# Sampling stage in loops, causal filter merged with the step sizes, a scan product on VectorE

## The chip, the cores and the metric

The kernel runs on one core of a Trainium2 chip. The metric is the device time of one execution in microseconds. TensorE (PE) multiplies, VectorE (DVE), ScalarE (ACT) and GpSimd (POOL) do the element work, and SyncE (SP) issues most transfers.

## The reference

Two layers work on an image x of shape (2, 128, 64, 64).

Layer 0 normalises over the channels and runs four deformable convolutions with kernels 1, 1, 3 and 7 wide, together 60 taps. Every tap samples the image at a learned place:

```python
offset = conv2d(x, off_w, off_b, pad)
mask = 2.0 * jax.nn.sigmoid(conv2d(x, mod_w, mod_b, pad))
py = base_y + off[:, :, 0]
px = base_x + off[:, :, 1]
sampled = bilinear_sample(x, py, px) * mask[:, None]
return jnp.einsum('bckhw,ock->bohw', sampled, reg_w.reshape(O, C, k * k))
```

The offsets and masks come from ordinary convolutions. The four results and a pooled branch are normalised and fused, and a mixture of 8 experts follows.

Layer 1 normalises, projects to 512 channels, filters them with a 5x5 depthwise kernel, and applies channel and spatial attention. Half of the channels (256) go through a causal filter of four taps along the 4096 positions, SiLU, and a selective scan with 16 states: delta = softplus(projection), state = exp(delta * A) * state + delta * u * B, y = sum over states of C * state. The result is gated and projected, and a layer of 64 specialists closes.

## The kernel before

**Sampling.** `deformable` takes the 8192 positions in 16 groups of 512 (four tiles of 128). For each of the 60 taps of a group, GpSimd issues four indirect gathers (L641) of table rows into one of four corner slots. VectorE and ScalarE weigh the four corners and add them up (L671 to L687 on VectorE, L953 on ScalarE), TensorE transposes the result (`turn`, L868), ScalarE copies that to SBUF (L961, `operands`), and TensorE multiplies it with the tap's weights (`multiply`, L879), which SyncE loads tap by tap (L580). Multiplication runs two taps behind (LAG). VectorE lists the row numbers of a later tap (L695, `list_rows`), on which GpSimd's next gathers wait.

In between, the positions of later groups are made: ScalarE stages seven shifted patches of a strip (`stage`), TensorE filters them with the 49 taps of the offset and mask convolution (`convolve`, L856), ScalarE sorts the sums (`sort`), and VectorE computes positions, indices, factors and weights at fixed taps. The order on every engine is written out by hand: constants such as SORT_AT, STAGE_AT and CONV_AT say behind which tap each step stands. `group_loop` unrolls the 16 groups; within one, two short loops (LOOPS) cover taps 2 to 25 and 26 to 45. TensorE's program is unrolled over all groups and taps:

```python
for half, c in ((0, g + 2), (1, g + 1), (1, g + 2)):
    begin, end = CONV_AT[half]
    ...
    if c < GROUPS and begin <= at < end:
        convolve(c, half, at - begin, end - begin)
```

Group 15 leaves out what would prepare a next group, and group 14 half of it.

**Layer 1.** For each of the two batches, `causal` loads all of u (two halves of 2 MB), filters it on VectorE (L2149 the first tap, L2152 the others) and applies SiLU on ScalarE (L2164). Its block ends, and `step_sizes` starts: in eight chunks of 512 positions TensorE projects, ScalarE makes exp and log (softplus), VectorE replaces the log by a polynomial where the argument is small (L2324 to L2336), forms delta (L2339) and delta * u (L2345), and TensorE and ScalarE turn the product into `dut`. Then `scan` goes over 4 chunks of 1024 positions times 16 states, 64 steps: ScalarE scales eight tiles of `dut` by B (L2422) and makes two decays (L2427), TensorE turns the products into the drive (L2506), VectorE scans both halves (L2477) and keeps the carries (L2462), GpSimd multiplies with C (L2444), and TensorE adds up (L2520). VectorE keeps the chunk's sum with L2467.

## Time and profile before

| | us |
|---|---|
| median of 3 runs (lowest, highest) | 9125.77 (9112.52, 9134.54) |
| the profiled execution | 9135.6 |
| its span | 9133.6 |
| mean granted TensorE clock | 0.812 |
| sampling stage (207 to 6600) | 6393 |
| causal filter and step sizes, batch 0 (7710 to 7860) | 150 |
| scan, batch 0 (7860 to 8209) | 349 |

The time is that of the whole execution, the span that from the first to the last instruction. A busy share tells how long an engine worked; idle time of an engine means something only where others wait for it.

### The profile page before, as it was taken

The numbers are of one execution on the slowest core, as the hardware profiler recorded it, in microseconds if no ns is written. First come the engines' busy times: TensorE is split into PE (matmuls) and PEld (weight loads), VectorE is DVE, ScalarE is ACT, GpSimd is POOL, SyncE is SP. The second block draws the span as 40 slices with busy tenths as digits, with TensorE's granted clock in tenths as the row PEclk, the third lists the DMA queues.
The fourth block names the chain that finished last, engine by engine and source line by source line (L and its number), as shares of the span: only waits on it lengthen the run. The fifth ranks groups of instructions, "written<-read, shape, count | busy, mean of one in ns | idle before, by whom it ended". The sixth has DMA issues, their size and how long they took to land. (4 is left out here: it accounts for less than half of the span.)

```text
span 9133.6 us, 99111 instructions
## 1 busy us (share of the span) xinstructions
PE 5511.6 (60%) x22734; PEld 3442.0 (38%) x22734; DVE 5304.2 (58%) x10463; ACT 4537.0 (50%) x11966; POOL 4809.8 (53%) x4571
## 2 busy tenths in 40 slices
PE   4665555555555555555556565554478985665757
PEld 4433333333333333333333333322235432462644
DVE  3454554555555555545555555555527886887962
ACT  1444444544444454444445444444452664895940
POOL 1555555655556565555556565555500884481830
PEclk9877777878788788777777787777799997896977
DMA  6565666666666666655566666666640001131234
GB/s 167 168 194 169 180 181 180 189 179 191 180 190 186 182 194 189 182 172 177 169 182 192 181 198 182 183 185 196 180 157 27 28 28 38 57 107 68 99 134 149
DMA packets 587069, 1413.87 MB, mean 155 GB/s; under 512 B 93923, under 2 KB 258032, under 8 KB 581616
## 3 DMA queue, kind: packets, MB, share of 16 engines
q0 software_dynamic: 308224, 1006.95, 37.7%
q1 hardware_dynamic: 276210, 398.68, 13.7%
q10 hardware_dynamic: 2304, 4.20, 0.1%
q8 instruction: 164, 2.69, 0.1%
q14 instruction: 167, 1.37, 0.1%
HBM read 1323.03 MB, written 85.86 MB: 154 GB/s over the span
## 5 line engine op out<-in xcount | busy, mean ns | idle before, releaser
L641 POOL DMA_INDIRECT st_corners<-corner_table,df_rows x3840 | 3648.5, 950 | 2809.2 <-DVE df_rows L695 1562.2
L868 PE MATMUL df_turn_ps<-main_ident,df_sampled 128*128 128x128 f32 x3840 | 729.2, 322 | 2667.4 <-ACT df_turned L961 1353.0
L879 PE MATMUL df_acc_ps<-df_turned,df_tapw 128*128 128x512 f32 x3840 | 2100.3, 675 | 90.0 <-issue 43.3
L682 DVE TENSOR_TENSOR st_corners<-st_corners,df_part_ps 128x512 f32<-128x512 f32 x960 | 660.6, 688 | 2550.4 <-ACT df_part_ps L953 1969.4
L961 ACT ACTIVATE df_turned<-df_turn_ps 128x512 f32<-128x512 f32 x962 | 562.8, 585 | 2512.6 <-remote 2049.8
L868 PEld LDWEIGHTS df_turn_ps<-main_ident,df_sampled 128*128 128x128 f32 x3840 | 515.3, 164 | 3412.8 <-issue 1857.5
L953 ACT ACTIVATE df_part_ps<-st_corners,df_share 128x128 f32<-128x128 f32 x3840 | 1191.2, 356 | 401.6 <-DVE df_sampled L687 236.7
L953 ACT ACTIVATE st_corners<-st_corners,df_share 128x128 f32<-128x128 f32 x3840 | 1218.9, 391 | 43.1 <-DMA st_corners<-corner_table,df_rows 24.7
L856 PE MATMUL df_conv_ps<-st_ow,df_patch 128*128 128x147 f32 (+1 forms) x6272 | 1150.8, 338 | 26.9 <-issue 26.9
L856 PEld LDWEIGHTS df_conv_ps<-st_ow,df_patch 128*128 128x128 f32 x6272 | 1048.7, 230 | 35.0 <-issue 34.2
L879 PEld LDWEIGHTS df_acc_ps<-df_turned,df_tapw 128*128 128x128 f32 x3840 | 783.8, 223 | 707.7 <-issue 634.5
L2444 POOL TENSOR_TENSOR sc_read<-sc_state,sc_c_row 128x1024 f32<-128x1024 f32 x256 | 601.3, 2372 | 476.3 <-DVE sc_state L2477 409.3
L687 DVE TENSOR_TENSOR df_sampled<-st_corners,df_part_ps 128x512 f32<-128x512 f32 x960 | 660.3, 688 | 287.8 <-remote 182.3
L677 DVE TENSOR_TENSOR df_part_ps<-st_corners,df_weight_ps 128x512 f32<-128x512 f32 x960 | 683.2, 712 | 39.1 <-issue 39.1
L671 DVE TENSOR_TENSOR st_corners<-st_corners,df_weight_ps 128x512 f32<-128x512 f32 x960 | 653.8, 681 | 26.7 <-issue 12.0
L683 DVE TENSOR_TENSOR df_part_ps<-st_corners,df_part_ps 128x512 f32<-128x512 f32 x960 | 661.6, 689 | 0.0
L2477 DVE TENSOR_TENSOR_SCAN sc_state<-sc_decay,sc_carry,sc_drive_ps 128x1024 f32<-128x1024 f32 x256 | 594.1, 2341 | 68.9 <-PE sc_drive_ps L2506 44.4
L1843 PE MATMUL dw_conv_ps<-dw_padded,dw_diag 128*128 128x512 f32 x1024 | 471.3, 613 | 12.1 <-DVE dw_u L1968 12.1
L1953 DVE SCALAR_TENSOR_TENSOR dw_conv_ps<-dw_padded,dw_dw_w,dw_conv_ps 128x512 f32<-128x512 f32 x576 | 383.4, 749 | 104.4 <-PE dw_conv_ps L1843 104.4
L1821 POOL TENSOR_TENSOR dw_aside<-dw_aside,dw_scaled 128x512 f32<-128x512 f32 x320 | 407.3, 1273 | 47.6 <-POOL dw_aside L1821 1.3
L2422 ACT ACTIVATE sc_product<-l1i_dut,l1s_bt 128x256 f32<-128x256 f32 x1024 | 421.0, 494 | 0.5 <-DVE sc_a L2456 0.5
L2506 PE MATMUL sc_drive_ps<-main_ident,sc_product 128*128 128x128 f32 x2048 | 278.0, 280 | 207.6 <-ACT sc_product L2422 195.5
(319 smaller groups left out, 5537.7 us busy)
## 6 DMA issues: line engine op xcount, KB each, us to landing
df_tapw<-in_tap_w_dram SPq DMA_DIRECT2D x962, 128.0 KB
sc_c_row<-c SPq DMA_DIRECT2D x128, 512.0 KB, 3.7
st_corners<-corner_table,df_rows POOLq DMA_INDIRECT x3840
y_b<-df_y SPq DMA_DIRECT2D x128, 256.0 KB, 2.7
f_y_in<-y_b SPq DMA_DIRECT2D x128, 256.0 KB, 4.1
l1f_w<-in_w_dram SPq DMA_DIRECT2D x32, 1024.0 KB, 6.9
corner_table<-st_corners SPq DMA_DIRECT2D x16, 1024.0 KB
u<-dw_u SPq DMA_DIRECT2D x64, 256.0 KB, 2.1
```

The costliest lines, as they stand in the source:

```text
L641: nc.gpsimd.indirect_dma_start(corners[slot][:, j].rearrange("p v c -> p (v c)"), None, table, bass.IndirectOffsetOnAxis(ap=rows[slot][:, ...
L671: nc.vector.tensor_tensor(near, near, w[:, :, 0:2, :], ALU.mult).then_inc(weighed_v, 1)
L677: nc.vector.tensor_tensor(part_ps[:, 0:VT], corners[slot][:, 0:VT, 2:4, :], w[:, :, 2:4, :], ALU.mult).then_inc(weighed_v, 1)
L682: nc.vector.tensor_tensor(left, left, part_ps[:, :, 0, :], ALU.add).then_inc(paired, 1)
L683: nc.vector.tensor_tensor(part_ps[:, :, 1, :], corners[slot][:, :, 1, :], part_ps[:, :, 1, :], ALU.add).then_inc(paired, 1)
L687: nc.vector.tensor_tensor(sampled[pair][:], left, part_ps[:, :, 1, :], ALU.add).then_inc(summed, 1)
L856: m = nc.tensor.matmul(conv_ps[:, second, 0:n], patch[:, kx, row * W:(row + 2) * W], ow_sb[:, ky, kx, 0:n], start=False, stop=closes, skip ...
L868: t = nc.tensor.transpose(turn_ps[pair][:, j * TILE:(j + 1) * TILE], sampled[pair][:, j, :], ident[:])
L879: m = nc.tensor.matmul(acc_ps[:, h, :], tapw[pair][:, h * P:(h + 1) * P], turned_sb[pair][:], start=first, stop=last, skip_group_check=not ...
L953: nc.scalar.activation(dst, src, ACT.Copy, scale=share[slot][:, j - VT, v:v + 1]).then_inc(weighed_a, 1)
L2444: nc.gpsimd.tensor_tensor(read[2 * s + h][:], state[2 * s + h][:], c_row[s][:], ALU.mult).then_inc(read_done, 1)
L2477: v.tensor_tensor_scan(out=state[2 * s + h][:], data0=decay[2 * s + h][:], data1=drive_ps[h][:], initial=carry[:, bass.ds(n, 1), h], op0=A ...
```

## The change

The sampling stage's groups become loops on every engine, eight pairs of groups, with the taps' loops inside. TensorE gets a loop over 16 groups with three taps, a loop of two halves of 22 taps, and 11 taps. It filters for the next group, one half of the strip in each half of the stretch, in 18 taps each, one output row at a time, and waits once for all seven patches. The multiplications of the last two taps come at the end of their own group, before the next group's first turn. Sorting, staging and counting stand at other taps, the strip is loaded later in the group, and the last groups are no longer exempt. `causal` and `step_sizes` become one block, `filter_and_steps`: u comes in quarters, SiLU of the first quarter is followed by the first two chunks' projections, the polynomial lies in PSUM, and GpSimd forms delta * u. In the scan VectorE scales the eighth tile of each state, two states ahead.

```diff
-    SORT_AT = (53, 6 * SLOTS + 1)
-    STAGE_AT = (6 * SLOTS + 1, 54)
+    SORT_AT = (6 * SLOTS + 1, 11 * SLOTS + 1)
+    STAGE_AT = {1: 6 * SLOTS + 1, 0: 52}
-    CONV_AT = {0: (27, 53), 1: (-5, 25)}
-    POSITION_AT, INDEX_AT, FACTOR_AT, COUNT_AT, WEIGHT_AT = 47, 49, 51, 53, 56
+    STRETCH, HEAD, SHARES = 22, 3, 9
+    POSITION_AT, INDEX_AT, COUNT_AT, FACTOR_AT, WEIGHT_AT = 47, 49, 51, 53, 56
...
-            for g in range(GROUPS):
-                ring = g % 2
-                tap = 0
+            with eng.Fori(0, GROUPS // 2) as q:
+                with eng.Fori(0, 2) as ring:
+                    g = 2 * q + ring
+                    tap = 0
...
             def serve(b, gl, nb, ngl):
 
                 g = b * GPB + gl
-                if nb < B:
-                    sp.wait_ge(strip_free, g + 2)
-                    load_strip(nb, ngl)
                 tap = LAG
...
                     tap += rounds * SLOTS
+                sp.wait_ge(strip_free, g + 2)
+                load_strip(nb, ngl)
                 for tap in range(tap, TAPS):
...
-                if g + 1 == GROUPS:
-                    return
...
-            def convolve(c, half, part, parts):
+            def convolve(c, half, second, part, parts):
+
+                share = -(-len(conv_taps) // parts)
+                if part == 0:
+                    if not second:
+                        pe.wait_ge(patched, KMAX * (2 * c + half + 1))
...
+                for ky, kx in conv_taps[part * share:(part + 1) * share]:
...
+            with pe.Fori(0, GROUPS) as g:
+                for tap in range(HEAD):
                     turn(g, tap, tap % 2)
...
                     if tap >= LAG:
                         known(g, tap - LAG)
...
+                with pe.Fori(0, 2) as half:
+                    for u in range(STRETCH):
+                        pair = (HEAD + u) % 2
+                        tap = half * STRETCH + (HEAD + u)
+                        turn(g, tap, pair)
+                        if 2 <= u < 2 + 2 * SHARES:
+                            convolve(g + 1, half, (u - 2) // SHARES, (u - 2) % SHARES, SHARES)
+                        multiply(g, tap - LAG, pair, g * (TAPS // 2) + half * (STRETCH // 2) + (HEAD + u - LAG) // 2)
+                for tap in range(HEAD + 2 * STRETCH, TAPS):
+                    turn(g, tap, tap % 2)
+                    known(g, tap - LAG)
+                for tap in range(TAPS - LAG, TAPS):
+                    known(g, tap)
...
-def causal(nc, tag, d, b, u_dram, conv1_sb, xs_sb):
...
-def step_sizes(nc, tag, d, b, ident, xs_sb, delta_sb, dut_sb, bt_sb, c_dram):
+def filter_and_steps(nc, tag, d, b, ident, u_dram, conv1_sb, xs_sb, delta_sb, dut_sb, bt_sb, c_dram):
...
-        poly = [sb(f"poly{h}", [P, SPAN]) for h in range(HALVES)]
+        poly = [pb(f"poly{h}", [P, SPAN]) for h in range(HALVES)]
...
+            load_u(0)
+            sp.dma_start(conv_b[:], d["conv1_b"]).then_inc(loaded, 16)
...
+            for q in range(1, PARTS):
+                load_u(q)
...
+            silu(0)
             keep_low(0)
             soften(0)
             keep_low(1)
             soften(1)
+            for q in range(1, PARTS):
+                silu(q)
...
+            for q in range(PARTS):
+                dve.wait_ge(u_loaded[q], 16 * HALVES)
+                for k in range(CONV1):
+                    for h in both:
...
+        @block.gpsimd
+        def _(pool):
+            for c in range(GPB):
                 if c >= 2:
-                    dve.wait_ge(turned, 2 * (c - 1))
-                for h in both:
-                    dve.wait_ge(stepped, HALVES * c + h + 1)
-                    v.tensor_tensor(du[s][:, h, :], delta_sb[:, h, cols(c)], xs_sb[:, h, cols(c)],
-                                    ALU.mult).then_inc(driven, 1)
+                    pool.wait_ge(turned, 2 * (c - 1))
+                for h in range(HALVES):
+                    pool.wait_ge(stepped, HALVES * c + h + 1)
+                    nc.gpsimd.tensor_tensor(du[c % 2][:, h, :], delta_sb[:, h, cols(c)], xs_sb[:, h, cols(c)],
+                                            ALU.mult).then_inc(driven, 1)
...
-                for j in range(TPC):
+                for j in range(LAST):
                     t = ch * TPC + j
...
+            def multiply(ch, n, s):
+                t = ch * TPC + LAST
+                v.tensor_scalar(product[s][:, LAST, :], dut_sb[:, t, :], bt_sb[:, t, bass.ds(n, 1)], None,
+                                ALU.mult).then_inc(multiplied_v, 1)
...
+                if not isinstance(n, int) or n + 2 < STATES:
+                    multiply(ch, n + 2, s)
+                elif ch + 1 < CHUNKS:
+                    multiply(ch + 1, n + 2 - STATES, s)
...
-                    pe.wait_ge(multiplied, (k + 1) * TPC)
+                    pe.wait_ge(multiplied, (k + 1) * LAST)
+                    pe.wait_ge(multiplied_v, k + 1)
```

## Rows read from the trace of the kernel before

**Rows 1.** Stretches: busy us of PE, PEld, DVE, ACT, POOL; clock; DMA share; GB/s.

```profile
207.00:6600.00 6393.00, 3603.73 (x13532) 2226.73 (x13532) 3467.57 (x7157) 3021.70 (x9097) 3639.47 (x3831) 0.78 0.62 184
...
7710.00:7860.00 150.00, 66.61 (x160) 24.36 (x160) 113.79 (x179) 83.09 (x115) 0.00 (x0) 0.59 0.08 31
7860.00:8209.00 349.00, 241.19 (x2048) 223.96 (x2048) 309.28 (x265) 339.07 (x642) 300.55 (x128) 0.99 0.28 97
```

**Rows 2.** The page's costliest groups of instructions, whole span.

```profile
L879 PE MATMUL df_acc_ps<-df_turned,df_tapw 128*128 128x512 f32 x3840 | 2100.3, 675 | 90.0 <-issue 43.3
...
L1821 POOL TENSOR_TENSOR dw_aside<-dw_aside,dw_scaled 128x512 f32<-128x512 f32 x320 | 407.3, 1273 | 47.6 <-POOL dw_aside L1821 1.3
```

**Rows 3.** Waits of 1000 to 6000 us: total us, times, longest.

```profile
ACT df_turned L961 <- remote: 1643.0, 159, 18.5
...
POOL st_corners L641 <- DVE df_rows L695: 1196.5, 216, 16.7
...
POOL st_corners L641 <- issue: 855.0, 2705, 2.0
```

**Rows 4.** GpSimd's timeline of a sampling cycle: start, us, what, idle before.

```profile
1099.66 0.95 POOL L641 DMA_INDIRECT st_corners<-corner_table,df_rows  x1 [0.30 <-issue]
1109.32 0.95 POOL L641 DMA_INDIRECT st_corners<-corner_table,df_rows  x1 [8.71 <-DVE df_rows L695]
```

**Rows 5.** Table of stretches, groups 1, 6, 13 and 15 of the sampling stage.

```profile
607.00:1025.00 418.00, 227.72 (x881) 146.46 (x880) 217.25 (x449) 190.46 (x571) 228.12 (x240) 0.75 0.60 176
2641.00:3019.00 378.00, 224.20 (x883) 141.51 (x881) 216.30 (x449) 188.94 (x571) 225.57 (x237) 0.82 0.65 191
5437.00:5830.00 393.00, 228.00 (x880) 145.56 (x880) 215.88 (x450) 189.86 (x571) 228.82 (x242) 0.78 0.64 188
6226.00:6585.00 359.00, 181.96 (x472) 79.71 (x472) 206.34 (x417) 175.60 (x536) 215.38 (x228) 0.76 0.66 195
```

**Rows 6.** Table of stretches for L687 alone, taps from 3 of groups 0, 1.

```profile
250.00:392.00 142.00, 15.45 (x23) 0.83 0.62 183
634.00:776.00 142.00, 13.75 (x20) 0.73 0.60 176
```

**Rows 7.** VectorE's timeline, causal filter and step sizes of batch 0.

```profile
7725.10 2.74 DVE L2149 TENSOR_SCALAR l1i_xs<-ca_u,l_conv 128x1024 f32<-128x1024 f32 x4 [12.74 <-DMA ca_bias<-in_conv_b_dram]
...
7744.76 14.43 DVE L2152 SCALAR_TENSOR_TENSOR l1i_xs<-ca_u,l_conv,l1i_xs 128x1024 f32<-128x1024 f32 x12
...
7773.09 0.95 DVE L2324 TENSOR_SCALAR ss_poly<-ss_e 128x512 f32<-128x512 f32 x2 [12.32 <-ACT ss_e L2290]
...
7815.57 0.88 DVE L2324 TENSOR_SCALAR ss_poly<-ss_e 128x512 f32<-128x512 f32 x2 [0.73 <-ACT ss_e L2290]
```

**Rows 8.** Groups of instructions in 7709 to 7860.

```profile
L2345 DVE TENSOR_TENSOR ss_du<-l1s_delta,l1i_xs 128x512 f32<-128x512 f32 x16 | 10.3, 685 | 0.0
...
L2164 ACT ACTIVATE l1i_xs<-l1i_xs,ca_bias 128x1024 f32<-128x1024 f32 x8 | 8.9, 1142 | 11.5 <-DVE l1i_xs L2152 11.4
...
L2324 DVE TENSOR_SCALAR ss_poly<-ss_e 128x512 f32<-128x512 f32 x16 | 6.7, 426 | 16.0 <-ACT ss_e L2290 15.7
```

**Rows 9.** Timelines of ScalarE, VectorE and GpSimd in the scan.

```profile
8501.16 3.29 ACT L2422 ACTIVATE sc_product<-l1i_dut,l1s_bt 128x256 f32<-128x256 f32 x8
...
8506.43 3.30 ACT L2422 ACTIVATE sc_product<-l1i_dut,l1s_bt 128x256 f32<-128x256 f32 x8
...
8502.67 0.13 DVE L2462 COPY sc_carry<-sc_state 128x1 f32<-128x1 f32 x1
8502.97 1.22 DVE L2467 COPY l1i_dut<-sc_y_ps 128x1024 f32<-128x1024 f32 x1 [0.17 <-PE sc_y_ps L2520]
...
8507.64 2.34 DVE L2477 TENSOR_TENSOR_SCAN sc_state<-sc_decay,sc_carry,sc_drive_ps 128x1024 f32<-128x1024 f32 x1
...
8509.94 2.34 DVE L2477 TENSOR_TENSOR_SCAN sc_state<-sc_decay,sc_carry,sc_drive_ps 128x1024 f32<-128x1024 f32 x1
...
8502.89 2.36 POOL L2444 TENSOR_TENSOR sc_read<-sc_state,sc_c_row 128x1024 f32<-128x1024 f32 x1 [0.57 <-issue]
```

More of the change, by code:

```diff
@@ L782, in after @@
                     count(g - 1, COUNT_LATE_AT[tap])
-                if tap == COUNT_AT:
-                    count(g, 0)
-                if g + 1 == GROUPS:
-                    return
                 if tap == POSITION_AT:
@@ L790, in after @@
                     indices(g + 1, 1 - ring)
+                if tap == COUNT_AT:
+                    count(g, 0)
                 if tap == FACTOR_AT:
@@ L849, in convolve @@
                     inner = 2 <= ky <= 4 and 2 <= kx <= 4
                     n = COLS if middle else c1 if inner else c3
-                    if ky == 0:
-                        pe.wait_ge(patched, KMAX * (2 * c + half) + kx + 1)
-                    for second in (1, 0):
-                        closes = middle and second == 0
-                        row = ky + 2 * second
-                        m = nc.tensor.matmul(conv_ps[:, second, 0:n], patch[:, kx, row * W:(row + 2) * W],
-                                             ow_sb[:, ky, kx, 0:n], start=False, stop=closes,
-                                             skip_group_check=not closes)
-                        if middle:
-                            m.then_inc(convolved, 1)
+                    row = ky + 2 * second
@@ L862, in turn @@
+                    m = nc.tensor.matmul(conv_ps[:, second, 0:n], patch[:, kx, row * W:(row + 2) * W],
+                                         ow_sb[:, ky, kx, 0:n], start=False, stop=middle,
+                                         skip_group_check=not middle)
+                    if middle:
+                        m.then_inc(convolved, 1)
             def turn(g, tap, pair):
@@ L927, in sort @@
                 k4, k3 = TAPS_OF[0], TAPS_OF[1]
-                if half == 0 and c > 0:
+                if half == 0 and not isinstance(c, int):
                     act.wait_ge(raw_free, c)
@@ L2188, in step_sizes @@
         bt_ps = pb("bt_ps", [P, TILES // B, STATES])
+        u_loaded = [sem(f"u_loaded{q}") for q in range(PARTS)]
+        cleared = sem("cleared")
+        tapped = sem("tapped")
+        active = sem("active")
         loaded = sem("loaded")
@@ L2266, in _, with silu @@
         def _(act):
-            act.wait_ge(loaded, 16 * 3)
+            act.wait_ge(loaded, 16 * 4)
             act.wait_ge(one_set, 1)
+            def silu(q):
+                for h in range(HALVES):
+                    act.wait_ge(tapped, (q + 1) * CONV1 * HALVES - HALVES + h + 1)
+                    part = xs_sb[:, h, q * LP:(q + 1) * LP]
+                    nc.scalar.activation(part, part, ACT.Silu, bias=conv_b[:, h:h + 1]).then_inc(active, 1)
             def keep_low(c):
```

178 lines of the change are left out of this document (70 added, 108 removed).

## The prediction

> **What bounds the kernel now.** I read the table of stretches first [rows 1]. 6393 of 9134 us are the sampling stage, and in it no engine works more than 57% of the time (GpSimd 3639, TensorE 3604, VectorE 3468, ScalarE 3022 us). So it is bound by a chain of waits. The stretch 7710 to 7860 is the causal filter and the step sizes of batch 0, 7860 to 8209 its scan; batch 1 has nearly the same lengths, so what is worked out for batch 0 counts twice. In the scan ScalarE is busy 339 of 349 us.
>
> The waits of the sampling stage come next [rows 3]: in 5000 us ScalarE stands 1643 us before the turned copy L961 in 159 waits, some 10 us each, and GpSimd stands 1197 us in 216 waits for the row lists L695. GpSimd's timeline shows the shape [rows 4]: gathers in bursts (0.95 us each), the last of a burst at 1099.66, the next burst only at 1109.32, 8.71 us later. In a burst the gathers follow each other every 1.25 us, 20 us for the 16 of four taps; with the pause that is 28.4 us for four taps. A group of 60 taps takes 401 us on average ((6585−207−359)/15 by the bounds in [rows 1, 5], the last group's 359 left out), but single ones 378 and 418 us for the same instructions. I could not find in the trace what makes ScalarE stand; the spread is a property of the chain, and it is the largest unknown here.
>
> **The sampling stage.** *The last group.* Before, group 15 leaves out all that prepares a next group. It takes 359 us against 393 of group 13, two before it [rows 5], and it has 472 matmul records against 880. In loops every group does the same, so group 15 now filters, sorts and computes positions for a group that doesn't exist. Term: +36 us (34 by that pair, 42 against the mean of 401; the low side since filters alone, half of which group 14 lacks, cost little).
>
> *The ends of the groups.* Five engines now jump back over a whole group 16 times, and TensorE also once inside each. What a long jump costs, no row shows. Below it is nothing, when it falls into one of the long waits of [rows 3], which most of the boundary is; above, the nearest row is GpSimd's longest gap without a releaser, 2.0 us (855.0 us in 2705 gaps, 0.3 each) [rows 3]; with two engines of the chain jumping in turn that is 4 us. TensorE also now multiplies taps 58 and 59 before it turns tap 0 of the next group, where it had turned first. These multiplies wait for ScalarE's copies L961 of those taps, which ScalarE issues only behind the weighing of taps 0 and 1. Behind them stand turn 0 and turn 1, and VectorE's sum L687 of tap 2 waits for turn 0. A multiply is 4 records of 675 ns [rows 2], 2.7 us, so two are 5.4 us above and nothing below, because the gather of tap 2 (5 us of issue behind tap 1) is awaited anyway. I take 0.5 for the jumps and 1.0 for the order: 1.5 us × 16 = +24 us; ends 0 and (4 + 5.4) × 16 = 150.
>
> The Trainium skill, "Runtime: NRT & Kernel Launch", § Instruction fetch mechanics, says that a taken branch to a place outside the two pages at hand makes the engine wait for a fetch, and therefore favours unrolling. That speaks against this edit; no row of this kernel isolates it, and it is the rule behind the second rival below.
>
> *The filter sums.* Their records per group stay about the same, but stand as 12 for each of 36 taps (5 to 22 and 27 to 44) where it was mostly 8 for some 50 taps. Group 13 has 408 records more than group 15 and 46 us more of TensorE [rows 5], 0.11 us each, 1.4 us for 12; with a multiply's 2.7 and the turns this stays near or below the 5 us of a tap's gathers. One stretch of the kernel before already has 12 records per tap: taps 3 to 24 of group 0. In 142 us from 250 on, VectorE makes 23 sums L687; in 142 us at the same place of group 1, with 8 records, 20 [rows 6]. So the denser filters don't slow the chain, and may loosen its bursts. But single groups differ by as much for no visible reason. Bounds: all groups as the fastest (378) or the slowest (418) [rows 5], (−23 or +17) × 16 = −370 or +270; I take −20, and a third of the bounds for the range.
>
> *Moved steps.* ScalarE sorts the second half at tap 45, one tap after TensorE's last share of it; VectorE wants the offsets at tap 47. Two taps at its running pace are some 7 us; the sort is seven short copies. It is covered, with about 4 us to spare; if not, VectorE stands in its positions, and the row lists of four taps later and with them GpSimd's next burst are late, up to 4 us × 16 = 64. Behind a late sort on ScalarE stands the weighing of tap 46, for which L682 waits. SP's strip load moves from the group's head to behind the load of tap 46: the strip is free since tap 25 and read first at tap 52, so SP doesn't stand and the tap loads behind it are two taps early. The wait for all seven patches instead of each costs nothing: they are staged one group or 20 taps earlier. Swapping count and factors moves 1.3 us of VectorE work within its own waits: 0.
>
> **The merged stage, twice.** On VectorE's timeline [rows 7] the first filter op starts at 7725.10, after 12.74 us of waiting for the whole input of 4 MB (half 0 first, then the bias behind both); the filter ends at 7744.76 + 14.43 = 7759.2; the first polynomial starts at 7773.09. Now a quarter of each half (1 MB together) is enough to start; a quarter of the transfer is some 3 of the 12.7 us, plus a fixed part: I take 7 saved (0 to 9). All filtering (34.1 us) stays in front of the first polynomial, but the first quarter's SiLU, projection and softplus run under it: the gap of 13.9 us goes. Then chunks come each 10.6 us (four from 7773.09 to 7815.57), with 0.73 idle. VectorE loses the two products L2345 (2 × 0.685 us [rows 8], 1.3) to GpSimd (2 × 1.27 [rows 2]); the first polynomial step L2324 writes PSUM and rises from 426 ns [rows 8] to about the 685 of L2345, +0.5. VectorE is then at 10.6 − 0.7 idle − 0.8 = 9.1 us per chunk, ScalarE at (83.1 busy [rows 1] − 8.9 SiLU [rows 8])/8 = 9.3 plus its waits. I take 9.9 a chunk: 8 × 0.7 = 5.6 us saved. One block barrier less I put at 0.8 us; the longer way through GpSimd adds 1.3 us once. Sum 7 + 13.9 + 5.6 + 0.8 − 1.3 = 26, twice: −52 us (ends −30 and −70: one stage of overlap failing, or the chunk reaching 9.3).
>
> **The scan, twice.** ScalarE has a period of 5.27 us per state (8501.16 to 8506.43), 3.29 of it eight products, 0.41 each, the rest two decays [rows 9]. With seven it is 4.86. On VectorE scan and carry follow at 2.30 us (8507.64 to 8509.94), 4.60 for two, and the copy L2467, 1.22 us and 8 times in a scan of 64 states, adds 0.15 [rows 9]. The eighth product there: a fourth of L2149's 128x1024 (4 in 2.74 us [rows 7]), 0.17, with some fixed part 0.25. That makes 5.0 for VectorE. GpSimd's reads are 2 × 2.36 = 4.72. The new period is that of VectorE, with a little slack 5.07: 5.27 − 5.07 = 0.2 × 128 states = −26 us (ends: −52, the whole product; 0, if the added op disturbs as much as it frees).
>
> **Sum.** −52 − 26 + 36 + 24 − 20 = −38 from the profiled execution's 9135.6 (span 9133.6): 9098. The median of runs is 9125.8, 10 lower; so 9088, rounded to 9090. Measurement tells 0.2%, 18 us, from no change.
>
> **Rivals.** (1) *GpSimd goes first.* VectorE's product comes right behind scan and carry, at the moment in which GpSimd reads: carry at 8502.67, GpSimd's read from 8502.89 for 2.36 us [rows 9]. Should the product have to wait out a read, scan and product make 4.60 + 2.36 + 0.25 = 7.2 a state, 1.95 over the present period: +250 us, against the −26 assumed, so 9088 + 276, about 9365. It decides once the product waits over 0.4 us. Against it: the copy L2467, though from PSUM, runs undisturbed in 1.22 us in the midst of such a read [rows 9]. The Trainium skill, "SBUF — State Buffer", § Who interferes with whom, says that a VectorE op in a two-port mode (tensor_scalar among them) and a GpSimd op exclude each other for the whole instruction, whoever issues first; L2149's speed fits that mode, and no run here shows the two together. If VectorE gets the gap between reads, the same lock costs 0.1 a state.
>
> (2) *The loops cost more than the merger saves.* With 4 us for the jumps and 3 for the order, 16 × 7 + 36 = +148, less 78: +70 on 9125.8, 9196. For it: chain-bound, every late turn is passed on; against: the boundary has the longest waits already. From 2.6 us per group on (42/16) nothing is gained. With late offsets on top 9260.
>
> (3) *The chain loosens.* If the groups go as group 0's stretch, a third of −370, −120 for −20: about 8990. For: [rows 6]; against: group 6 took only 378 us with 8 records [rows 5].
>
> (4) *The scan doesn't move*, a full engine swapped for another: 9115.
>
> **Chances.** Forecast, within 9045 to 9107: 0.37. (3) 0.13. (4), with small mixes around no change: 0.14. (2) 0.22. (1) 0.14. So faster 0.50, same 0.14, slower 0.36. The range, 8960 to 9280, reaches a third of the upper bound of the bursts with (2), and leaves out (1) and the far end of (3). The likeliest case alone is 9045 to 9107.
>
> **What the profile after would show.** Batch 0's stretch from the end of attention to the first scan 124 us instead of 150, the first filter op 6 us after its block begins, no 12 us gap before the first polynomial. Scan 335 instead of 349 us, ScalarE's products seven, VectorE idle near 15 us; for rival 1, gaps of over a microsecond before the new product with GpSimd as neighbour. Group lengths near 401, the last one near 395 and not 359; for rival 2 longer gaps between taps 59 and 2 of each group. What would make all of it wrong is a shift between the burst patterns: 10 us per group is 160 us.

## The result and the profile after

The changed kernel takes 9063.2 us (median of 20 runs, 9027.4 to 9095.4) against 9141.1 us for the kernel before in the same comparison (20 runs, 9102.0 to 9231.7): ratio 0.991, 95% interval 0.989 to 0.993. The forecast was 9090, a fall of 36 us; measured are 78. The direction was right and the time lies in the range of the likeliest case. The terms behind it were not all right: merger and scan together gave some 13 us less than forecast, and the sampling stage gained where a loss of 40 us was forecast.

The profiled execution after spans 9037.2 us, 96.4 less than before. It is one of the shorter of the 20 (9039.1 against the median of 9063.2), so some 20 us of the 96 belong to that execution and not to the change. First the table of stretches of the changed kernel: sampling group 0, groups 13 and 15, the merged stage and the scan of batch 0. The columns are those of [rows 1]; the merged stage's stretch ends here at the first scan instruction, where that of [rows 1] ended 7.5 us before it, at the clearing of the carries.

```profile
217.00:616.00 399.00, 241.09 (x872) 145.53 (x872) 217.26 (x449) 189.60 (x570) 233.48 (x247) 0.76 0.63 184
5374.00:5768.00 394.00, 244.27 (x880) 143.39 (x880) 217.33 (x449) 191.72 (x573) 228.31 (x242) 0.78 0.64 188
6165.00:6552.00 387.00, 236.42 (x872) 145.22 (x872) 214.32 (x442) 187.17 (x563) 213.24 (x225) 0.79 0.61 180
7681.00:7816.00 135.00, 70.29 (x171) 27.98 (x172) 108.07 (x168) 91.11 (x127) 19.95 (x16) 0.59 0.12 42
7816.00:8147.00 331.00, 257.16 (x2039) 228.51 (x2037) 327.52 (x325) 308.36 (x567) 303.61 (x128) 0.97 0.28 99
```

Against [rows 5], group 15 now has as many matmul records as the others and takes 387 us instead of 359. In the scan VectorE has gone from 309 to 328 us of work and is the fullest engine, with ScalarE down from 339 to 308 [rows 1].

Where the 96.4 us of the profile pair lie, by the first and last instructions of the stages: the first sum L687 (now L690) comes at 216.4 instead of 206.9 (+9.4); from there to the first sum of group 15 it is 5948.6 instead of 6019.4 (−70.8); group 15 itself takes 386.9 to its last sum instead of 358.3 (+28.6). So the sampling stage gains 32.8. From the end of attention's last transfer to the first TENSOR_TENSOR_SCAN it is 135.3 instead of 157.8 (−22.5), between the scans 195.4 instead of 215.6 (−20.2), each scan, from the start of its first TENSOR_TENSOR_SCAN to that of its last, 322.9 and 322.8 instead of 333.7 and 333.8 (−10.8 and −11.0), and the rest is +0.9. Merger 43, scan 22, sampling 33 less.

The merged stage on VectorE's timeline of the changed kernel, batch 0 (start, length, what, idle before):

```profile
7688.82 1.42 DVE L2300 TENSOR_SCALAR l1i_xs<-ss_u,l_conv 128x1024 f32<-128x1024 f32 x2 [5.68 <-DMA ss_u<-u]
...
7722.83 1.28 DVE L2312 TENSOR_SCALAR ss_poly<-ss_e 128x512 f32<-128x512 f32 x2
...
7743.02 1.29 DVE L2312 TENSOR_SCALAR ss_poly<-ss_e 128x512 f32<-128x512 f32 x2 [2.03 <-ACT ss_e L2255]
...
7764.14 1.29 DVE L2312 TENSOR_SCALAR ss_poly<-ss_e 128x512 f32<-128x512 f32 x2 [2.72 <-ACT ss_e L2255]
...
7793.67 1.29 DVE L2312 TENSOR_SCALAR ss_poly<-ss_e 128x512 f32<-128x512 f32 x2 [0.16 <-ACT ss_e L2255]
...
7808.57 0.09 DVE L2449 MEMSET sc_carry<- 128x32 f32 x1 [5.78 <-PEq L2115]
```

The wait for u fell from 12.74 to 5.68 us, and the first polynomial starts with no gap behind the filter; both as forecast (for before see [rows 7]). But from the first polynomial to the scan's first instruction it is still 85.7 us (7722.83 to 7808.57), where it had been 86.9 (7773.09 to 7860.03). The last chunk's polynomial starts at 7793.67 here, 70.8 us behind the first, and in the kernel before at

```profile
7846.30 0.88 DVE L2324 TENSOR_SCALAR ss_poly<-ss_e 128x512 f32<-128x512 f32 x2 [0.23 <-ACT ss_e L2290]
```

which is 73.2 us behind the first. So the eight chunks gained 2.4 us, and the way from the last polynomial to the scan grew from 13.7 to 14.9. ScalarE's waits in these stretches, before and after:

```profile
ACT ss_v L2284 <- PE ss_delta_ps L2237: 10.6, 13, 2.2
ACT l1i_dut L2299 <- PE ss_dut_ps L2251: 7.4, 2, 7.2
```

```profile
ACT l1i_dut L2264 <- PE ss_dut_ps L2210: 8.3, 3, 7.8
ACT ss_v L2249 <- PE ss_delta_ps L2196: 5.9, 9, 1.3
ACT ss_low L2241 <- PE ss_dut_ps L2210: 3.5, 2, 2.5
```

They add up to 18.0 and 17.7 us. The SiLU of the last three quarters now lies in this stretch as well:

```profile
7726.45 6.34 ACT L2233 ACTIVATE l1i_xs<-l1i_xs,ss_conv_b 128x1024 f32<-128x1024 f32 x6
```

The scan of the changed kernel, VectorE then GpSimd:

```profile
7982.87 1.21 DVE L2462 COPY l1i_dut<-sc_y_ps 128x1024 f32<-128x1024 f32 x1
7984.00 1.51 DVE L2466 TENSOR_SCALAR sc_product<-l1i_dut,l1s_bt 128x256 f32<-128x256 f32 x1
...
7990.03 0.38 DVE L2466 TENSOR_SCALAR sc_product<-l1i_dut,l1s_bt 128x256 f32<-128x256 f32 x1
...
7994.93 0.42 DVE L2466 TENSOR_SCALAR sc_product<-l1i_dut,l1s_bt 128x256 f32<-128x256 f32 x1
7995.27 2.33 DVE L2477 TENSOR_TENSOR_SCAN sc_state<-sc_decay,sc_carry,sc_drive_ps 128x1024 f32<-128x1024 f32 x1
```

```profile
7982.98 2.38 POOL L2439 TENSOR_TENSOR sc_read<-sc_state,sc_c_row 128x1024 f32<-128x1024 f32 x1 [1.00 <-DVE sc_state L2477]
7987.90 4.74 POOL L2439 TENSOR_TENSOR sc_read<-sc_state,sc_c_row 128x1024 f32<-128x1024 f32 x2 [2.54 <-issue]
7992.83 4.75 POOL L2439 TENSOR_TENSOR sc_read<-sc_state,sc_c_row 128x1024 f32<-128x1024 f32 x2 [0.19 <-DVE sc_state L2477]
```

The product that starts at 7984.00 finds a GpSimd read at work since 7982.98. It is recorded at 1.51 us and ends at 7985.51, 0.15 behind the read's end (7985.36). The one at 7994.93 starts 2.10 us into a read of 2.37 and lasts 0.42: it too ends 0.15 behind the read. Of the 128 products 124 start inside a read, and 9 in 10 of them end between 0.149 and 0.156 us after it. So each of these 124 products waits for GpSimd's read. It costs little because it stands where the read is nearly over: the one at 7994.93 holds VectorE for 0.34 us, while one with no read beside it, before the first scan, holds it for 0.26. A state takes 4.93 us in most cases (the median). Three of the 64 states, those at a chunk's start, take 8.3: they hold two copies of 1.21 us, and the product behind the second finds a read that has just begun, as at 7984.00. The average is 5.09; in the kernel before it was 5.26. VectorE now works without a gap from the first scan instruction to the last.

### The profile page after: what moved, and what is told of

Read it like the earlier page. It is cut to its first block and busy times, and to the rows that moved or that the text cites. A ratio compares the mean times of both kernels' runs of the same rounds, so it can differ in the third digit from the quotient of the medians.

```text
span 9037.2 us, 105713 instructions
## 1 busy us (share of the span) xinstructions
PE 5819.1 (64%) x23134; PEld 3547.4 (39%) x23134; DVE 5350.8 (59%) x10585; ACT 4510.1 (50%) x11874; POOL 4845.0 (54%) x4603
## 3 DMA queue, kind: packets, MB, share of 16 engines
q1 hardware_dynamic: 278226, 399.68, 13.7%
## 5 line engine op out<-in xcount | busy, mean ns | idle before, releaser
L873 PE MATMUL df_acc_ps<-df_turned,df_tapw 128*128 128x512 f32 x3840 | 2300.3, 725 | 447.3 <-issue 273.5
L862 PEld LDWEIGHTS df_turn_ps<-main_ident,df_sampled 128*128 128x128 f32 x3840 | 543.8, 168 | 2491.0 <-issue 1773.2
L850 PE MATMUL df_conv_ps<-st_ow,df_patch 128*128 128x147 f32 (+1 forms) x6664 | 1178.5, 327 | 318.5 <-issue 317.8
L873 PEld LDWEIGHTS df_acc_ps<-df_turned,df_tapw 128*128 128x128 f32 x3840 | 819.6, 232 | 1198.3 <-issue 1045.2
L690 DVE TENSOR_TENSOR df_sampled<-st_corners,df_part_ps 128x512 f32<-128x512 f32 x960 | 660.0, 687 | 378.3 <-remote 261.6
L2417 ACT ACTIVATE sc_product<-l1i_dut,l1s_bt 128x256 f32<-128x256 f32 x896 | 370.5, 497 | 7.4 <-PE sc_drive_ps L2513 6.9
```

The source lines that it names most:

```text
L690: nc.vector.tensor_tensor(sampled[pair][:], left, part_ps[:, :, 1, :], ALU.add).then_inc(summed, 1)
L850: m = nc.tensor.matmul(conv_ps[:, second, 0:n], patch[:, kx, row * W:(row + 2) * W], ow_sb[:, ky, kx, 0:n], start=False, stop=middle, skip ...
L862: t = nc.tensor.transpose(turn_ps[pair][:, j * TILE:(j + 1) * TILE], sampled[pair][:, j, :], ident[:])
L873: m = nc.tensor.matmul(acc_ps[:, h, :], tapw[pair][:, h * P:(h + 1) * P], turned_sb[pair][:], start=first, stop=last, skip_group_check=not ...
```

## The experiments

The kernels ran on several chips. In the first measurement and for "denser filters" the kernel before took about 9145 us, for all the others, on three chips, about 7565. Every ratio is to the kernel before on the same chip at the same time. Below, "the slower kind" and "the faster kind" stand for the two. One of the three fast chips was measured twice and gave 7568 both times; the slow result of "denser filters" comes from a fourth chip, and that of the first measurement from one that isn't named. That it is the chip, and not something else that differs between the measurements, is therefore likely and not shown.

| run | us | kernel before | ratio (95% interval) |
|---|---|---|---|
| merger only | 7527.7 | 7568.1 | 0.9947 (0.9934 to 0.9961) |
| scan product only | 7543.0 | 7568.1 | 0.9972 (0.9961 to 0.9983) |
| sampling edits only | 7582.4 | 7568.1 | 1.0018 (1.0009 to 1.0027) |
| changed, groups unrolled | 7516.5 | 7568.1 | 0.9933 (0.9919 to 0.9946) |
| changed, unaltered | 7504.8 | 7560.0 | 0.9924 (0.9911 to 0.9938) |
| first filters by column | 7498.0 | 7560.0 | 0.9915 (0.9901 to 0.9928) |
| two products on VectorE | 7780.6 | 7560.0 | 1.0297 (1.0281 to 1.0312) |
| product behind the first scan | 7511.1 | 7560.0 | 0.9930 (0.9915 to 0.9946) |
| last group spared, first filters by column | 7492.7 | 7559.9 | 0.9909 (0.9894 to 0.9924) |
| delta * u on VectorE | 7503.0 | 7559.9 | 0.9926 (0.9913 to 0.9940) |
| denser filters | 9046.6 | 9149.2 | 0.9882 (0.9845 to 0.9920) |
| sampling edits only, again | 7580.3 | 7568.5 | 1.0015 (1.0006 to 1.0024) |

**The parts alone.** Three kernels take the kernel before and give it one part of the change each, the functions of the diff taken over whole.

```diff
-                causal(nc, f"ca{b}", d, b, u_dram, conv1_sb, xs_sb)
...
+                    filter_and_steps(nc, f"ss{b}", d, b, ident, u_dram, conv1_sb, xs_sb, delta_sb, dut_sb, bt_sb,
+                                     c_dram)
```

> The kernel before with the merged causal filter and step sizes alone. My theory from the two profiles: the stretches from the end of attention to the first scan and between the two scans shrink by 22.5 and 20.2 us (batch 0 and 1), so the whole is 43 us shorter, ratio 0.995. Rival: the merger is worth more, and the sampling stage nothing: ratio 0.993 or less.

It took 7527.7 us, 40 less, which agrees with the 43 of the profile pair. The rival's 0.993 lies just outside the interval.

```diff
-                for j in range(TPC):
+                for j in range(LAST):
...
+            def multiply(ch, n, s):
```

> The kernel before with the eighth product on VectorE alone. My theory: 22 us shorter (11 in each scan, as in the profile after), ratio 0.9975, with the period per state at 4.94 us. Rival: the product costs more where the stages around it are the old ones; then the period stays near 5.2 us and nothing is gained.

It took 7543.0 us. The ratio of 0.9972 is 21 us, and its scans last 323.6 and 322.7 us instead of 333.7 and 333.8: the gain belongs to the scan alone.

```diff
-            for g in range(GROUPS):
-                ring = g % 2
+            with eng.Fori(0, GROUPS // 2) as q:
+                with eng.Fori(0, 2) as ring:
...
+                        if 2 <= u < 2 + 2 * SHARES:
+                            convolve(g + 1, half, (u - 2) // SHARES, (u - 2) % SHARES, SHARES)
```

> The kernel before with the sampling stage's edits alone (loops, order of the filter sums, moved steps). The forecast had +40 us here. The two profiles show 33 us less, the medians leave about 13 us less (78 less 43 and 22). My theory now: between 0 and 35 us shorter, ratio 0.996 to 1.0. Rival, the forecast's own sum: 40 us longer, ratio 1.004, and the merger and the scan are worth more than the profiles show.

It took 14 us more than the kernel before, ratio 1.0018, so both expectations missed for this chip: neither a gain nor 40 us. Some 8 to 9 of the 14 us are the later first sum (215.2 us, against 207.0 and 205.9 in the two kernels above). Why the forecast's other terms don't act shows in the stretches. First the kernel before with the merger, its group 1 and group 15; then this kernel's same groups.

```profile
508.00:808.00 300.00, 210.90 (x880) 126.18 (x880) 224.31 (x449) 189.70 (x571) 226.89 (x241) 0.93 0.80 245
4716.00:5011.00 295.00, 178.16 (x472) 79.35 (x472) 209.78 (x416) 175.42 (x534) 217.94 (x231) 0.84 0.80 241
```

```profile
520.00:822.00 302.00, 216.10 (x881) 126.74 (x880) 224.81 (x450) 190.23 (x571) 228.77 (x241) 0.91 0.80 244
4736.00:5029.00 293.00, 215.03 (x870) 127.62 (x868) 219.56 (x442) 185.53 (x560) 216.88 (x229) 0.90 0.79 241
```

A group takes 300 us here, not 401: 60 taps of 5.0 us, which is what GpSimd takes to issue a tap's four gathers, one every 1.25 us. The last group, with 398 matmul records more, is no longer than before. On such a chip the issue of the gathers bounds the stage, and the extra work is hidden behind it.

**The waits on the two kinds of chip.** The waits between 208 and 5010 us of the kernel before with the merger, where it takes 7528 us:

```profile
PEld df_turn_ps L868 <- issue: 2152.4, 1022, 9.6
ACT st_corners L953 <- DMA st_corners<-corner_table,df_rows: 1558.8, 812, 3.5
PE df_turn_ps L868 <- DVE df_sampled L687: 1429.6, 786, 9.4
POOL st_corners L641 <- issue: 1042.2, 3421, 0.3
```

ScalarE's wait for something unnamed before L961, the largest of [rows 3], is gone, and GpSimd never pauses over 0.3 us. On the slower kind that wait is long. This is the pause of [rows 4] in the kernel before, TensorE then ScalarE:

```profile
1089.23 1.88 PE L879 MATMUL df_acc_ps<-df_turned,df_tapw 128*128 128x512 f32 x4
1104.12 1.12 PE L868 MATMUL df_turn_ps<-main_ident,df_sampled 128*128 128x128 f32 x4 [13.00 <-ACT df_turned L961]
```

```profile
1103.46 0.60 ACT L961 ACTIVATE df_turned<-df_turn_ps 128x512 f32<-128x512 f32 x1 [15.03 <-remote]
```

TensorE had ended all its work by 1091.1, the turn included, and ScalarE's copy of that turn starts only at 1103.46. In the program that copy waits for signals of TensorE alone. In the whole stage 241 of these copies wait over 3 us, 2416 us together, and half of them start over 6.6 us behind TensorE's last matmul; in the changed kernel it is 261, 2319 us together. Where the kernel before takes 7565 us, there is one such wait. So TensorE's result reaches ScalarE late on the slower kind.

A second difference can be seen at 205 us, before the first turn. TensorE's timeline of the kernel before in the execution of 9136 us, then of the kernel before with the merger in that of 7520 us:

```profile
204.76 2.20 PE L856 MATMUL df_conv_ps<-st_ow,df_patch 128*128 128x147 f32 x16
208.70 0.28 PE L856 MATMUL df_conv_ps<-st_ow,df_patch 128*128 128x147 f32 x1 [1.74 <-issue]
211.53 0.40 PE L856 MATMUL df_conv_ps<-st_ow,df_patch 128*128 128x147 f32 x1 [2.54 <-issue]
214.32 0.40 PE L856 MATMUL df_conv_ps<-st_ow,df_patch 128*128 128x147 f32 x1 [2.40 <-issue]
```

```profile
188.61 25.01 PE L856 MATMUL df_conv_ps<-st_ow,df_patch 128*128 128x147 f32 x185
```

The same instructions run in one piece on the one, and on the other eight of them follow each other at 2.1 to 2.8 us. Such gaps, 1.2 to 3 us before a filter sum or a multiply and with no releaser, stand 26 times in the sampling stage of the kernel before (52 us together) and 203 times in that of the changed kernel (390 us), each time with packets of gathers on the way; the kernels on the faster kind whose traces were searched (merger only, changed, unrolled, sampling edits again) have none. Gathers alone don't bring them about: on the slower kind most matmuls run at full pace beside gathers too. Why signals come late and matmuls are held up there was not found. Nor is it shown whether the changed kernel has more of the gaps by its loops or by its order of sums.

**The loops.** The changed kernel with the groups written out again on the four engines:

```diff
-            with eng.Fori(0, GROUPS // 2) as q:
-                with eng.Fori(0, 2) as ring:
-                    g = 2 * q + ring
+            for g in range(GROUPS):
+                ring = g % 2
...
-            with pe.Fori(0, GROUPS) as g:
+            for g in range(GROUPS):
...
-                with pe.Fori(0, 2) as half:
+                for half in range(2):
```

> The changed kernel with the sampling stage's groups written out again on TensorE, VectorE, ScalarE and GpSimd, everything else of the change kept (order of the filter sums, steps, the last group's extra work). It prices the loops. The forecast's term: the loops cost 0.5 us a group, so this is 8 us faster than the changed kernel, ratio to it 0.999. Rival A: a long jump costs 4 us a group, this is 64 us faster. Rival B: the loops help, since TensorE fetches less code while gathers load the DMA engines (54 fetches of 16 KB against 164); then this is slower than the changed kernel by 20 us or more.

> The changed kernel itself, unaltered. On the chip of the runs before this one the kernel before took 7568 us, and the parts alone gave -40 (merger), -25 (scan) and +14 us (sampling). If the parts add up, this is 51 us faster than the kernel before there, ratio 0.9933, and the loops' price is the difference to the unrolled kernel's ratio, 0.9933: nothing. On a chip where the kernel before takes about 9140 us, I expect 0.991 as in the first measurement.

Unrolled 0.9933, in loops 0.9924 (another chip of the faster kind): the loops gain 7 us, with an uncertainty of 14, so they cost nothing that can be measured there. Rival A's 64 us are out, and rival B's 20 us stand at the edge of the interval. On the slower kind, where TensorE is held up, the loops were not tested alone. TensorE's code fetches, 54 of 16 KB in the changed kernel, are 167 again when unrolled, without effect on the time there. The parts add up: 40, 21 and −14 make 47, and the whole gives 57 by its ratio, with an interval of 47 to 67; unrolled, on the chip of the parts, it gives 51.

**The very first filters.**

```diff
             for half in range(2):
-                for second in range(2):
-                    convolve(0, half, second, 0, 1)
+                convolve_first(half)
```

> The changed kernel, but the filter sums of the very first group in the old order (by column of the filter, each column's work behind its own patch), before the loops. In the profiles the first tap of group 0 is summed 8 to 9 us later since the change. My theory: the wait for all seven patches stands in the first group's way, where nothing hides it; this gives back 8 us, on any chip. Rival: the late start has another cause (the order of rows, code loading), then it gives back under 2 us.

`convolve_first` goes by column of the filter, and each column waits only for its own patch. 7498.0 against 7504.8 us, 7 less, with overlapping intervals; but its first sum stands at 206.7 us again instead of 216.5. The new way costs 8 to 10 us once, at the start. The run puts back the separate waits and the old order of the sums together, so it doesn't tell the two apart.

**Two products.**

```diff
-    LAST = TPC - 1
+    LAST = TPC - 2
...
+                for j in range(LAST, TPC):
+                    t = ch * TPC + j
+                    v.tensor_scalar(product[s][:, j, :], dut_sb[:, t, :], bt_sb[:, t, bass.ds(n, 1)], None,
```

> The changed kernel with two products of each state on VectorE, one behind the other, and six on ScalarE. The trace after shows each product to end 0.15 us behind the end of the GpSimd read that runs when it starts. Theory A (exclusion, turns in order of asking): the first product waits for the read's end as now, GpSimd's next read has asked by then and goes before the second product, which waits 2.4 us: 7.3 us a state, 300 us slower in all. Theory B (exclusion, but VectorE keeps the turn): two products cost 0.6 us together, a period of 5.2, 35 us slower. Theory C (no exclusion, a slow op): the same 35 us, and products that end at no fixed distance from a read's end.

276 us slower than the changed kernel. A state takes 7.32 us (from 6449.11 to 6456.43). VectorE, then GpSimd:

```profile
6449.11 2.33 DVE L2478 TENSOR_TENSOR_SCAN sc_state<-sc_decay,sc_carry,sc_drive_ps 128x1024 f32<-128x1024 f32 x1
6451.36 0.12 DVE L2457 COPY sc_carry<-sc_state 128x1 f32 x1
6451.41 2.79 DVE L2467 TENSOR_SCALAR sc_product<-l1i_dut,l1s_bt 128x256 f32<-128x256 f32 x2
6454.12 2.33 DVE L2478 TENSOR_TENSOR_SCAN sc_state<-sc_decay,sc_carry,sc_drive_ps 128x1024 f32<-128x1024 f32 x1
6456.38 0.12 DVE L2457 COPY sc_carry<-sc_state 128x1 f32 x1
6456.43 2.33 DVE L2478 TENSOR_TENSOR_SCAN sc_state<-sc_decay,sc_carry,sc_drive_ps 128x1024 f32<-128x1024 f32 x1
```

```profile
6449.30 4.74 POOL L2439 TENSOR_TENSOR sc_read<-sc_state,sc_c_row 128x1024 f32<-128x1024 f32 x2 [2.57 <-DVE sc_state L2478]
6456.62 4.74 POOL L2439 TENSOR_TENSOR sc_read<-sc_state,sc_c_row 128x1024 f32<-128x1024 f32 x2 [2.57 <-DVE sc_state L2478]
```

The first product waits for the end of the read that runs (0.26 us); the next read, already asking, goes before the second product, which waits it out, lasts 2.46 us by itself and ends at 6454.2, 0.15 behind the reads' end. Theory A holds: 300 us foretold, 276 measured, and a state at 7.32 us as foretold. The two engines exclude each other in this pair of operations, and take turns.

**The product elsewhere.**

```diff
                     if isinstance(n, int) and n == 0 and ch > 0:
                         keep_y(ch - 1, h)
+                    if h == 0:
+                        if not isinstance(n, int) or n + 1 < STATES:
+                            multiply(ch, n + 1, 1 - s)
```

> The changed kernel with the product behind the first scan of a state, not the second, one state ahead. There GpSimd is between two reads (its only pause in a state, 0.19 us, is there). Theory A (exclusion): VectorE is first, the product takes its bare length of 0.25 to 0.3 us instead of 0.41, and GpSimd's read starts behind it; the period stays 4.9 (GpSimd's two reads with the product between them), the whole within 15 us of the changed kernel. If GpSimd is first instead, the product lasts over 2 us and the whole is 250 us slower. Theory C (no exclusion): the product lasts 0.41 us here as well.

7511.1 us, within 7 of the changed kernel, as theory A had it for the whole. For the single product it was only partly right. In 26 of 128 states it falls into the change from one read to the next and is short (0.33 to 0.35 us):

```profile
6461.57 0.34 DVE L2466 TENSOR_SCALAR sc_product<-l1i_dut,l1s_bt 128x256 f32<-128x256 f32 x1
6461.83 2.34 DVE L2477 TENSOR_TENSOR_SCAN sc_state<-sc_decay,sc_carry,sc_drive_ps 128x1024 f32<-128x1024 f32 x1
```

There it holds VectorE for 0.26 us. In 96 it has slid into a read's end again, 0.39 to 0.45 long, and in 6 it lasts 1.5 us or more, behind a copy of the chunk's sum. VectorE has hardly a gap (1.6 us in the whole scan): two scans with their carries at 2.30 us make, with a short product (0.26), the 4.86 us that these states take, and with a waiting one (0.34) the 4.93 of the others. So the product costs nearly the same wherever it stands.

**The last group spared.** The unrolled kernel, in which group 15 leaves out everything for a next group (and the first filters are by column):

```diff
+                        if 2 <= u < 2 + 2 * SHARES and g + 1 < GROUPS:
...
+                if g + 1 == GROUPS:
+                    return
```

> The changed kernel with two edits: the sampling groups written out again so that group 15 leaves out all work for a next group, and the very first filter sums by column as in the run before. Theory: where gathers bound the groups (a kernel before of 7560 us) the last group has nothing to give, since it takes 293 us with that work and 295 without; so only the 7 us of the first filter sums come back, ratio to the kernel before 0.991 to 0.992. Where the kernel before takes 9140 us, the last group gives back 28 us more, ratio 0.987. Rival: the last group's extra work costs on every chip, ratio 0.988 or less here too.

7492.7 us, 0.9909: 12 us below the changed kernel's 7504.8 of another chip of the faster kind, 5 of them beyond the first filters, which the intervals don't separate from 0. Its time is the lowest of all here where gathers bound the groups, though not clear of the changed kernel's by the intervals. Where the last group costs 28 us it wasn't run.

**delta * u on VectorE.**

```diff
+                for h in both:
+                    dve.wait_ge(stepped, HALVES * c + h + 1)
+                    v.tensor_tensor(du[s][:, h, :], delta_sb[:, h, cols(c)], xs_sb[:, h, cols(c)],
+                                    ALU.mult).then_inc(driven, 1)
...
-        @block.gpsimd
```

> The changed kernel with delta * u back on VectorE in the merged stage, the rest unaltered. The forecast let a chunk fall from 10.6 to 9.9 us, by ScalarE's pace; the trace after shows 10.1 to 10.6 us in pairs, with ScalarE waiting for TensorE twice in a chunk. Theory: the product's place on GpSimd lengthens the way from delta to the turned product and gives back what VectorE gains; this kernel is within 6 us of the changed one in either direction, ratio to it 0.999 to 1.001, VectorE without gaps in the chunks. Rival: VectorE would be the bound at 10.4 us a chunk plus its waits, 15 us longer in both batches together.

7503.0 us, the changed kernel's time (7504.8). VectorE's first polynomial step comes every 10.24 us, and VectorE works without a gap between:

```profile
6209.98 1.28 DVE L2312 TENSOR_SCALAR ss_poly<-ss_e 128x512 f32<-128x512 f32 x2
...
6220.22 1.28 DVE L2312 TENSOR_SCALAR ss_poly<-ss_e 128x512 f32<-128x512 f32 x2
...
6230.47 1.27 DVE L2312 TENSOR_SCALAR ss_poly<-ss_e 128x512 f32<-128x512 f32 x2
```

With the product on GpSimd VectorE's own work is 9.28 us a chunk, but the chunks come in pairs, one at 9.3 and one at 10.7 to 12, since VectorE waits 2.0 to 2.7 us for ScalarE in every second one: 10.1 on average. The stretch from the first polynomial to the scan is 85.8 us with the product on VectorE and 85.1 with it on GpSimd, both on the faster kind. What VectorE gave up it spends waiting for ScalarE, and the way from the last polynomial to the scan is 0.8 us longer: this part of the merger is worth nothing that can be measured.

**Denser filters.**

```diff
-    STRETCH, HEAD, SHARES = 22, 3, 9
+    STRETCH, HEAD, SHARES = 22, 3, 6
```

> The changed kernel with each half's filter sums in 12 taps instead of 18: 18 records of matmul per tap. The forecast held that denser filters don't slow the chain. Theory: a tap's work on TensorE is then some 0.6 + 18 x 0.14 + 1.9 = 5.0 us, about the 5.0 of a tap's gathers; where gathers bound the groups, nothing changes (ratio to the changed kernel 0.999 to 1.002), where TensorE's signals come late during gathers (a kernel before of 9140 us), the group lengths move by several us, in a direction I can't tell. Rival: TensorE becomes the bound in these 24 taps and every group is 10 us longer, 160 us in all.

This one ran where the kernel before takes 9149 us: ratio 0.9882, against 0.991 for the changed kernel in the first measurement. The intervals overlap. Its groups take 396.0 us on average, those of the changed kernel 396.6. Even at 18 records a tap the filters don't bound the stage there; the rival's 160 us are out. Nor do denser filters help, as the forecast had hoped.

> The kernel before with the sampling stage's edits alone once more, in the hope of a chip where the kernel before takes about 9140 us, as it did in the first measurement and in the run before this one. There: the whole change gave 78 us, the merger and the scan give 65 of them by the parts, so 13 us less are left for the sampling edits, ratio 0.9985; the profile pair says 33 us less, 0.9965. The forecast said 40 us more, 1.0044. On a chip where it takes 7560 us: 14 us more, as before.

It ran where the kernel before takes 7568 us and took 12 more, ratio 1.0015, as in the first such run. What the sampling edits alone do on the slower kind stays a difference: 78 us less 43 and 22, about 13 gained, with some 20 us of uncertainty from the ratio's interval. Whether they gain there at all is not shown by a run.

## Why the prediction was right, and where not

**The merger.** −52 forecast, −43 in the profile pair, −40 alone. Right in mechanism; the term mis-sized is the chunk. The input's wait gave 7.1 (7 forecast) and the gap 13.9, but the stretch from the first polynomial to the scan shrank by 1.2 us and not by the 4.3 that 5.6 for the chunks less 1.3 for the way through GpSimd make. The chunks gave 2.4 us. They began at 10.5 us on average and not at 10.6, a reading of the first four intervals alone, and they came to 10.1 and not 9.9: "ScalarE at 9.3 plus its waits, I take 9.9" lets ScalarE's waits shrink without a reason, and they are as long as before (18.0 and 17.7 us in the stretch). The SiLU of three quarters, 6.3 us of ScalarE that the sum left out, now stands there too, and the second chunk, prepared ahead, pays for it (ScalarE works 68.7 us in the stretch before and 67.2 after). The 1.3 us for GpSimd were right (13.7 to 14.9).

**The scan.** −26 forecast, −22 measured. The forecast let a state fall from 5.27 to 5.07 us with the copies L2467 spread over all states; on that footing it fell from 5.26 to 5.09. The price of the product was 0.25; bare it is 0.26, in its place 0.34. VectorE has 3.5 us idle in the scan's 331, where the forecast's picture of the profile after had near 15. Rival 1 has the right mechanism and nearly the right price: it came true in the kernel with two products, where the second one waits for a whole read and a state is 2.4 us longer. Its chance of 0.14 rested on who gets the turn, and VectorE's single product gets it, because it asks before the next read does. The Trainium skill, "SBUF — State Buffer", § Who interferes with whom, states the exclusion; the traces agree, with 0.15 us from the read's end to the product's.

**The last group.** +36 forecast, +28.6 in the profile pair. The mechanism is right for the slower kind; on the faster one it is −2 us, since there GpSimd's issue bounds the group.

**The ends of the groups.** +24 forecast. On the faster kind the loops' part is nothing that can be measured (0.9933 against 0.9924); on the slower it was not separated. From the last tap's sum to tap 2's, the 960 starts of the sum give 26.0 us a group after and 31.6 before, −5.6 × 15 = −84, where I had +1.5 each; taps 25 to 47, which now hold all of a half's filters, are 5.7 us a group longer and take it back (+85). The trace of the kernel with denser filters, also on the slower kind, has nearly the same (25.3 us, and 150.8 for taps 25 to 47). On the faster kind the boundary is 20.3 against 19.8. The order of the last multiplies was priced; the filter sums, which leave the boundary for these taps, were not. That they make the difference is the likely reading; no run moves them alone. The upper price of a multiply, 4 × 675 ns, was also too high: its four records overlap, and where nothing holds them up they take 1.9 us.

**The start.** Two terms were missed. "The wait for all seven patches instead of each costs nothing: they are staged one group or 20 taps earlier" was wrong for the first group, where it costs 9.4 us (the run by column gives them back, together with the old order). And TensorE no longer filters half 0 of group 1 before the first turn. That work had held up group 0, whose first sum stood 39.7 us before that of its tap 2, now 10.2: −29.5 us on the slower kind, where eight of those very matmuls crawl, and −6.3 on the other (16.1 to 9.8). I had counted the records of a group, and not those in front of the first.

**The filters.** −20 forecast for density, a guess from one stretch of group 0 [rows 6]. Taps 2 to 25 went from 148.3 to 147.3 us a group, 25 to 47 from 145.4 to 151.1, and 47 to 59 from 74.7 to 72.8; single groups differ by more than such steps (378 to 420 us before), and the kernel with denser filters is no faster a group. No gain by density is to be seen.

Together the sampling stage was forecast at +40 and came out near −13 to −33 on the slower kind of chip and +12 to +14 on the other. There the 36 us of the last group and the 24 of the boundaries have nothing to act on. The direction of the whole was carried by the merger and the scan, which hold on both. That the time fell into the forecast's 9045 to 9107 is in part luck: the sampling term was off by some 50 us, of which merger and scan take back 13, and the kernel before took 9141 us in this comparison and not the 9126 that the forecast started from, another 15. The view that bounds the sampling stage by its chain was a reading of the slower kind of chip only.

## What to carry to other kernels

Before an operation goes to VectorE beside a busy GpSimd, see in the trace where GpSimd's operation stands when it starts: one short product near a read's end costs 0.08 us more than its bare 0.26, a second behind it a whole read (2.4 us). Moving work off the fullest engine pays only up to the pace of the next one: the product that left VectorE in the merged stage was worth nothing, because ScalarE's work and its waits for TensorE set the pace there. Work ahead of a loop counts apart from work in it: two terms that were missed lay in front of the first group. And a bound that is read from one trace may belong to that chip; where an engine waits for long on a result that was ready, measure on another chip before the bound is used in a sum.

## What the runs showed of the hardware

The same program takes 7565 us on some chips and 9145 on another, 21% more, nearly all of it in the sampling stage (300 against 401 us a group; for the changed kernel all but 6 of 1533 us). On the slower one ScalarE starts on TensorE's results late (241 waits of over 3 us in the stage, against one), and TensorE in some stretches issues one matmul in 2.1 to 2.8 us while gathers move, where it otherwise runs at 0.14 us each. VectorE's 128x256 product and GpSimd's 128x1024 product exclude each other; a product that has to wait is recorded as longer, not later (2.46 us instead of 0.34 behind a whole read), and ends 0.15 us behind the read. Sixteen passes of a long loop on each engine, with 32 shorter ones inside it on TensorE, cost nothing that could be measured on the faster kind (7 us less than unrolled, give or take 14).
